# A depthwise convolution moved from TensorE to three other engines in a ternary feed-forward stage

## The chip, the cores and the metric

One Trainium2 chip, one of its cores, one launch. The metric is the device time of that core in microseconds (us), the median of several executions. Engines are TensorE (PE; its weight loads are PEld), VectorE (DVE), ScalarE (ACT), GpSimd (POOL) and SyncE (SP, which only issues transfers here).

## What is computed

Two gated blocks, each a cross attention and a feed-forward, are applied to `x` of 8 rows (batch entries) x 224 tokens x 512. The change is in the first feed-forward, which after a layer norm computes for each row:

```python
def bit_linear(x, w):      # x rounded to 8 bits per token, w to -1, 0, 1
    xq = act_quant(x)      # round(x * s) / s, s = 127 / max|x| of the token
    wq = weight_quant(w)   # clip(round(w / m), -1, 1) * m, m = mean|w|
    return einsum('bsd,hd->bsh', xq, wq)
h = bit_linear(x, w1)                        # 512 -> 2048 channels
h = depthwise_conv1d(h, conv_w, conv_b)      # 3 taps over the tokens, per channel
h = silu(h)
x = x + tanh(g) * bit_linear(h, w2)          # 2048 -> 512
```

## The kernel before

The four stages (attention 0, `bit_ffn`, attention 1, `fp4_ffn`) run one after the other, with `x1`, `x2` and `x3` in device memory between them. Each engine has its own instruction stream in `bit_ffn` (L1346 to L1961), with semaphores between them, and each stream is strictly in the order in which it is written. There is a prologue for row 0 and then nine turns (L1444): turn b does the first half of row b, prepares the input of row b+1 and finishes row b-1. Turn 8 only finishes row 7.

The 2048 hidden channels lie on the 128 partitions in 16 chunks, with the 224 tokens along the free dimension, and go through the engines in 8 groups of two chunks. For group g of row b:

- PE `up_group` (L1892): 2 x 4 bf16 matmuls of 128x224 give the integer product of the ternary `w1q` and the rounded input `xqT`.
- DVE `group` (L1763): two products with the tokens' factors `dB` give `u` in f32.
- PE `conv_group` (L1906): 2 x 3 f32 matmuls with diagonal matrices `taps` (L1919) are the convolution. The profile shows each f32 matmul as two instructions.
- ACT: `t` = conv + bias and `th` = tanh of half of that (L1650, L1651), two chunks each.
- DVE `finish_group` (L1757), two groups later: `h` = (`th` + 1) * `t`, which is twice the Silu. The factor is taken out again in later constants.

Then, per row: DVE `row_maxima` (L1789) reduces `h` over the chunks in three pieces and joins them with maxima; PE turns the 128 maxima per token over (L1956); DVE `row_scales` (L1775) makes the scale of each token; PE (L1888) and ACT (L1669) spread it to all partitions as `sB`; POOL (L1588) multiplies `h` by `sB` in 8 products of two chunks; DVE `round_hidden` (L1795) rounds it to bf16 in two halves; PE's `down` matmuls (L1947) are 32 of 128x512; DVE `add_residual` (L1801, L1807) gives the output.

The input of the next row is prepared in between, by DVE's `PREPARE` (L1722): `row_moments`, `normalise` (which waits for GpSimd's reciprocal roots, `row_roots`, L1549 to L1562), `input_maxima` (L1706 to L1711), `scale_input`, `round_input`, and `row_factors` (L1724). PE turns it over (L1872) and spreads the factors (L1881).

Before and in turn 0 the weights are rounded: ACT takes sums of absolute values (L1604), `total` (L1863) sums them over partitions, ACT and DVE round `w1` (L1607, L1741), POOL and ACT `w2` (L1577, L1664). ACT and POOL also make the diagonal matrices `taps` (L1616, L1571).

## Time and profile before

| | us |
|---|---|
| median of 3 runs | 2177.19 (2176.5 to 2177.56) |
| the profiled execution's own time | 2169.75 |
| its span, first to last instruction | 2168.0 |
| `bit_ffn`, first transfer issued to last residual | 716.1 to 1058.4 |
| `bit_ffn`'s first `up` matmul | 738.6 |
| mean granted TensorE clock | 0.953 |

The page gives each engine's busy time, which is an average over four stages with different limits. Only the stretch from 716 to 1059 us is touched by the change, so the rows below are from there. A line's group shows the idle time of its engine just before it and what ended it. A timeline lists instructions in the order of time, with repeated ones merged (x2 are two of them, and the duration is from the first's start to the last's end).

### The profile page before, as it was taken

The page shows a single profiled execution, that of the slowest core. Times are in us where ns is not written, and L with a number is a line of the kernel's source. Part 1 is how long each engine was busy: PE and PEld are TensorE (multiplying, and loading weights), DVE is VectorE, ACT ScalarE, POOL GpSimd, SP SyncE. Part 2 cuts the span into 40 slices and gives each one's busy share as a digit, 9 for nine tenths or more (in the row PEclk, how much of TensorE's full clock was granted, in tenths as well). Part 3 has the DMA queues.
Part 4 walks back from the last instruction along what each step waited for, and adds up shares of the span by engine and source line. Part 5 has one row for each costly group of instructions (what it writes and reads, how often), then busy time and mean ns, then how long its engine had stood idle before and what let it go on. Part 6 is the DMA issues. An engine that isn't in the chain of part 4 may idle for free. (4 is left out here: it accounts for less than half of the span.)

```text
span 2168.0 us, 42248 instructions
## 1 busy us (share of the span) xinstructions
PE 1926.6 (89%) x15174; PEld 1362.4 (63%) x15208; DVE 1480.5 (68%) x2752; ACT 948.0 (44%) x1305; POOL 1201.2 (55%) x1470
## 2 busy tenths in 40 slices
PE   5799999999987589899489999999999967899997
PEld 3467677777765478778255676767776754455553
DVE  4776776776765588988344666766766456889973
ACT  3176667776777653333123434434434432111110
POOL 3176776766764543323222667767766423877853
PEclk9899999999997799999699999999999988999998
DMA  7445444455420501110452444544543420010100
GB/s 206 106 114 133 113 123 121 117 124 123 115 72 18 198 10 45 31 42 18 153 142 75 115 130 141 148 140 128 149 142 115 161 85 10 30 37 30 34 29 24
DMA packets 184012, 208.67 MB, mean 96 GB/s; under 512 B 61481, under 2 KB 145705, under 8 KB 183337
## 3 DMA queue, kind: packets, MB, share of 16 engines
q1 hardware_dynamic: 183848, 206.46, 33.9%
q8 instruction: 107, 1.75, 0.4%
q14 instruction: 57, 0.46, 0.1%
HBM read 138.61 MB, written 67.53 MB: 95 GB/s over the span
## 5 line engine op out<-in xcount | busy, mean ns | idle before, releaser
L709 POOL TENSOR_TENSOR a_p_hl<-a_p,a_p_hl 125x448 bf16<-125x448 f32 x540 | 562.3, 1043 | 450.2 <-ACT a_p_hl L846 418.5
L836 ACT ACTIVATE a_p<-a_psum 125x1344 f32<-125x1344 f32 x192 | 247.9, 1291 | 135.0 <-PE a_psum L1248 127.9
L1014 DVE TENSOR_REDUCE a_nm<-a_psum 112x1 f32<-112x750 f32 x256 | 237.4, 934 | 98.9 <-PE a_psum L1268 98.3
L846 ACT ACTIVATE a_p_hl<-a_p 125x1344 bf16<-125x1344 f32 x192 | 254.0, 1323 | 81.9 <-PE a_psum L1286 78.3
L1286 PEld LDWEIGHTS a_psum<-a_v_st,a_p_hl 125*128 125x128 bf16 x4608 | 175.2, 98 | 40.5 <-issue 18.5
L1286 PE MATMUL a_psum<-a_v_st,a_p_hl 125*128 125x65 bf16 (+2 forms) x4608 | 186.6, 194 | 12.0 <-POOL a_p_hl L709 6.1
L1919 PE MATMUL f_conv<-f_u,f_taps 128*128 128x224 f32 x768 | 161.1, 359 | 22.4 <-DVE f_u L1771 21.7
L1158 PE MATMUL a_psum<-a_chl,a_w 128*128 128x375 bf16 x768 | 142.4, 331 | 22.8 <-DVE a_w L905 14.9
L1919 PEld LDWEIGHTS f_conv<-f_u,f_taps 128*128 128x128 f32 x768 | 141.6, 191 | 31.8 <-DVE f_u L1771 27.2
L1158 PE MATMUL a_psum<-a_chl,kept_w 128*128 128x375 bf16 x768 | 137.3, 332 | 23.1 <-DVE kept_w L905 18.0
L1268 PE MATMUL a_psum<-a_k_st,a_q_st 96*112 96x375 bf16 x512 | 128.1, 337 | 25.6 <-DVE a_nm L1014 19.0
L1158 PE MATMUL a_psum<-a_w,a_chl 128*125 128x512 bf16 x576 | 139.4, 384 | 8.4 <-DVE a_m_parts L995 5.7
L979 DVE TENSOR_TENSOR a_v_st<-a_psum,a_v_st 125x512 bf16<-125x512 f32 x96 | 66.0, 687 | 110.8 <-ACT a_v_st L814 110.8
L814 ACT ACTIVATE a_v_st<-a_psum 125x512 bf16<-125x512 f32 x96 | 58.3, 608 | 187.4 <-PE a_psum L1158 187.4
L1009 DVE CUSTOM_DVE_ANT_0 a_psum<-a_psum,a_mask_b 112x750 f32<-112x750 f32 x128 | 119.7, 940 | 26.6 <-PE a_psum L1268 25.2
L1158 PE MATMUL a_psum<-kept_w,a_chl 128*125 128x512 bf16 x576 | 134.7, 384 | 3.5 <-DVE a_q_tmp L976 3.4
L2244 POOL TENSOR_TENSOR f_ht<-f_ht,f_hp 128x512 f32<-128x512 f32 (+1 forms) x84 | 99.1, 1207 | 60.9 <-DVE f_hp L1997 59.8
L1268 PE MATMUL a_psum<-kept_k,a_q_st 128*112 128x375 bf16 (+1 forms) x512 | 123.1, 340 | 9.2 <-DMA kept_k<-a_k 4.3
L1650 ACT ACTIVATE f_t<-f_conv,f_cb 128x224 f32<-128x224 f32 x128 | 57.6, 450 | 166.8 <-PE f_conv L1919 166.8
L973 DVE TENSOR_TENSOR a_k_tmp<-a_psum,a_k_tmp 128x375 bf16<-128x375 f32 x128 | 69.7, 545 | 86.9 <-ACT a_k_tmp L807 86.7
L807 ACT ACTIVATE a_k_tmp<-a_psum 128x375 bf16<-128x375 f32 x128 | 61.7, 483 | 139.0 <-PE a_psum L1158 134.3
L1158 PEld LDWEIGHTS a_psum<-a_chl,kept_w 128*128 128x128 bf16 x768 | 73.1, 99 | 74.6 <-issue 34.2
(251 smaller groups left out, 4034.7 us busy)
## 6 DMA issues: line engine op xcount, KB each, us to landing
a_k<-a_k_tmp SPq DMA_DIRECT2D x64, 375.0 KB, 3.0
a_k_st<-a_k SPq DMA_DIRECT2D x96, 187.5 KB, 3.4
kept_k<-a_k SPq DMA_DIRECT2D x96, 187.5 KB, 3.4
a_c<-in_ctx_t SPq DMA_DIRECT2D x16, 750.0 KB, 6.1
ctx_parts<-a_chl SPq DMA_DIRECT2D x16, 750.0 KB, 9.7
a_chl<-ctx_parts SPq DMA_DIRECT2D x16, 750.0 KB, 6.0
a_q_st<-a_q SPq DMA_DIRECT2D x192, 56.0 KB, 2.2
rounded<-a_fw SPq DMA_DIRECT2D x24, 352.0 KB, 3.7
```

The costliest lines, as they stand in the source:

```text
L709: ins = nc.gpsimd.tensor_tensor(p_hl[0:MC, h % 2, 1, cols], p32[0:MC, h % 2, cols], p_hl[0:MC, h % 2, 0, cols], ALU.subtract)
L836: nc.scalar.activation(p32[0:MC, par, :].rearrange("p (b n) -> p b n", b=3), st[0:MC, :, 0:2 * S], ACT.Exp, scale=scale).then_inc(exp_done, 1)
L846: nc.scalar.activation(p_hl[0:MC, par, 0, :], p32[0:MC, par, :], ACT.Copy).then_inc(phi_done, 1)
L973: ins = nc.vector.tensor_tensor(k_tmp[:, cc % 2, 1, cols], bank[:, 0:MK], k_tmp[:, cc % 2, 0, cols], ALU.subtract)
L979: ins = nc.vector.tensor_tensor(v_st[0:MC, b.parity, k, :, DK + 1:VW], bank[0:MC, :].rearrange("p (h d) -> p h d", h=H), v_st[0:MC, b.pari ...
L1009: ins = nc.vector.tensor_tensor_reduce(out=sm_[0:HALF, 0:2, 0:MK], in0=sm_[0:HALF, 0:2, 0:MK], in1=mask_b[:, b.parity, s, :].rearrange("p ...
L1014: ins = nc.vector.tensor_reduce(out, sm_[0:HALF, 0:2, 0:MK], AX.XY, ALU.max, negate=True)
L1158: ins = nc.tensor.matmul(out, lhs, rhs, start=(c == 0 and n == 0), stop=(c == KC - 1 and n == 2))
L1268: ins = nc.tensor.matmul(sm_[0:HALF, kh, 0:MK], q_stack(b.parity, at(h), rows)[:, s * HALF:(s + 1) * HALF], k_stack(b.parity, at(h), rows) ...
L1286: ins = nc.tensor.matmul(ob[:, c0:c0 + width], p_hl[0:MC, h % 2, part, j * S + Q0[s]:j * S + Q0[s] + P], v_st[0:MC, b.parity, j, h, 0:widt ...
L1919: ins = nc.tensor.matmul(conv[:, g % 2, c * S:(c + 1) * S], taps[:, g * GC + c, k, :], u[:, g % 2, c, k:k + S], start=(k == 0), stop=(k == 2))
L2244: ins = nc.gpsimd.tensor_tensor(ht[:, cols], ht[:, cols], hp[:, cols], op)
```

## The change

In `bit_ffn` only:

- The input's values are no longer integers with a factor applied behind the matmul. `xn` is scaled and rounded on ACT (`scale_input`), brought back to its value with `dq` on DVE (`input_values`), and split into a bf16 half (`input_high`, ACT) and the bf16 rest (`input_low`, DVE). Both are turned over on PE (`turn_input`) and copied by ACT (`take_turned`). `up_group` runs both halves, 2 x 8 matmuls. The factors `dB`, their diagonal matmuls (L1881) and `row_factors` are gone.
- The convolution: ACT reads `up` from PSUM twice per chunk (`centre`): `t` = centre tap * `up` + bias, `left` = left tap * `up`. DVE adds the right tap's product in place (`add_right`, two instructions per group, reading `up`). POOL adds `left`, shifted by one token (`add_left`, one instruction per group). The matrices `taps`, `u`, `conv` and L1919 are gone; the taps times the mean of `w1` are `cws`.
- Silu: ACT's own (`silu`, one instruction per group), in place of tanh and `finish_group`.
- `up` has four PSUM banks in place of two. `row_maxima` takes four quarters. POOL's 8 products with `sB` stand between the `add_left` of groups 2 to 7. `row_roots(b+1)` stands behind `add_left(b, 0)` on POOL. ACT's `row_scales(b-1)` stands behind `silu(b, 0)`. PE's turning of the maxima stands behind `up_group(b+1, 0)`, and `down` is run in halves by q, with `turn_input(b+1, 1)` between them.
- At the start `total(0)` stands behind both `turn_input`s on PE, and the first scaling of `w2` is on DVE at the end of turn 0 instead of on POOL.

The diff, cut to its core:

```diff
+            def add_left(b, g):
+
+                pool.wait_ge(right_added, b * NG + g + 1)
+                row = t[:, g % RING, :, 1:S]
+                nc.gpsimd.tensor_tensor(row, row, left[:, g % RING, :, 0:S - 1], ALU.add).then_inc(left_added, 1)
+
+            def scale_hidden(b, par, n):
+
+                if n == 0:
+                    pool.wait_ge(sB_ready, b + 1)
+                part = h[:, par, 2 * n:2 * n + 2, :]
+                ins = nc.gpsimd.tensor_tensor(part, part, sB[:, :].unsqueeze(1).broadcast_to([P, 2, S]), ALU.mult)
+                if n % (QH // 2) < QH // 2 - 1:
+                    own.link(ins)
+                else:
+                    ins.then_inc(h_scaled, 1)
+
+            BEHIND = {2: (0, 1), 3: (2,), 4: (3,), 5: (4, 5), 6: (6,), 7: (7,)}
...
             def turn(b, par):
+                for g in range(NG):
+                    if in_range(b):
+                        add_left(b, g)
+                    if g == 0 and in_range(b + 1):
+                        row_roots(b + 1)
+                    if in_range(b - 1):
+                        for n in BEHIND.get(g, ()):
+                            scale_hidden(b - 1, 1 - par, n)
...
+            def scale_input(b):
+
+                act.wait_ge(inv_ready, b + 1)
+                for s in range(2):
+                    ins = nc.scalar.activation(xn[:, s, :], xn[:, s, :], ACT.Identity, bias=round_sb[0:HALF, 0:1],
+                                               scale=inv[:, s:s + 1])
+                ins.then_inc(xs_ready, 1)
+
+            def input_high(b):
+
+                act.wait_ge(xhat_ready, b + 1)
+                if not (isinstance(b, int) and b == 0):
+
+                    act.wait_ge(xT_ready, b * 2)
+                nc.scalar.activation(xq[:, 0, :, :], xn[:, :, :], ACT.Copy).then_inc(xhi_ready, 1)
...
+            def take_turned(b, part):
+
+                act.wait_ge(xT_ready, b * 2 + part + 1)
+                for s in range(2):
+                    ins = nc.scalar.activation(xqT[:, part, :, s * HALF:(s + 1) * HALF],
+                                               xT_ps[:, s * 512:s * 512 + KC * HALF].rearrange("p (c s) -> p c s", c=KC),
+                                               ACT.Copy)
+                ins.then_inc(xqT_ready, 1)
+
+            def centre(b, g):
+
+                n = b * NG + g
+                if not (isinstance(b, int) and n < RING):
+
+                    act.wait_ge(h_ready, n - RING + 1)
+                act.wait_ge(up_ready, n + 1)
+                for c in range(GC):
+                    ch = g * GC + c
+                    src = up[:, g % BANKS, c * S:(c + 1) * S]
+                    nc.scalar.activation(t[:, g % RING, c, :], src, ACT.Identity, bias=cb[:, ch:ch + 1],
+                                         scale=cws[:, ch, 1:2])
+                    ins = nc.scalar.activation(left[:, g % RING, c, 0:S - 1], src[:, 0:S - 1], ACT.Copy,
+                                               scale=cws[:, ch, 0:1])
+                ins.then_inc(centre_ready, 1)
+
+            def silu(b, par, g):
+
+                if g == 0 and not (isinstance(b, int) and b < 2):
+
+                    act.wait_ge(hq_ready, b * 2)
+                act.wait_ge(left_added, b * NG + g + 1)
+                nc.scalar.activation(h[:, par, g * GC:(g + 1) * GC, :], t[:, g % RING, :, :],
+                                     ACT.Silu).then_inc(h_ready, 1)
...
+            absolute_sum(0, 1, w1q)
+            scale_input(0)
+            absolute_sum(0, 2, w1q)
+            input_high(0)
+            absolute_sum(0, 3, w1q)
...
+            take_turned(0, 0)
+            take_turned(0, 1)
+            act.wait_ge(scale_ready, 1)
+            quantise_w1(ACT_W1[0])
+            quantise_w1(ACT_W1[1])
...
-                for g in range(NG if in_range(b) else 0):
-                    n = b * NG + g
+                for g in range(NG):
+                    if in_range(b):
+                        centre(b, g)
+                    if g >= 2 and in_range(b):
+                        silu(b, par, g - 2)
+                    if g == 2 and in_range(b - 1):
                         row_scales(b - 1)
+                    if g == 4 and in_range(b + 1):
+                        scale_input(b + 1)
+                    if g == 6 and in_range(b + 1):
+                        input_high(b + 1)
+                if in_range(b):
+                    silu(b, par, NG - 2)
                 if in_range(b + 1):
-                    prepare(b + 1)
+                    take_turned(b + 1, 0)
+                if in_range(b):
+                    silu(b, par, NG - 1)
+                if in_range(b + 1):
+                    take_turned(b + 1, 1)
...
+                nc.vector.tensor_scalar(dq[:, :], amax[:, :], 1.0 / 127.0, None, ALU.mult)
                 link(nc.vector.tensor_scalar(inv[:, :], inv[:, :], 127.0, None, ALU.mult))
-
-            def scale_input(b):
+                dve.sem_inc(inv_ready, 1)
...
+            def input_values(b):
+
+                dve.wait_ge(xs_ready, b + 1)
                 for s in range(2):
-                    ins = nc.vector.tensor_scalar(xn[:, s, :], xn[:, s, :], inv[:, s:s + 1], ROUND,
-            PREPARE = {1: row_moments, 2: normalise, 3: input_maxima, 4: scale_input, 5: round_input}
+                    ins = nc.vector.tensor_scalar(xn[:, s, :], xn[:, s, :], -ROUND, dq[:, s:s + 1], ALU.add, ALU.mult)
+                ins.then_inc(xhat_ready, 1)
+
+            def input_low(b):
+
+                dve.wait_ge(xhi_ready, b + 1)
+                nc.vector.tensor_tensor(xq[:, 1, :, :], xn[:, :, :], xq[:, 0, :, :], ALU.subtract).then_inc(xq_ready, 1)
+
+            PREPARE = {0: row_moments, 2: normalise, 3: input_maxima, 5: input_values, 7: input_low}
...
+            def add_right(b, g):
 
                 n = b * NG + g
-                if not (isinstance(b, int) and n < 2):
-
-                    dve.wait_ge(conv_ready, n - 1)
-                dve.wait_ge(up_ready, n + 1)
+                dve.wait_ge(centre_ready, n + 1)
+                if isinstance(b, int) and n == 0:
+                    dve.wait_ge(taps_ready, 1)
                 for c in range(GC):
-                    ins = nc.vector.tensor_tensor(u[:, g % 2, c, 1:S + 1], up[:, g % 2, c * S:(c + 1) * S],
-                                                  dB[:, :], ALU.mult)
-                ins.then_inc(u_ready, 1)
+                    ch = g * GC + c
+                    row = t[:, g % RING, c, 0:S - 1]
+                    ins = nc.vector.scalar_tensor_tensor(row, up[:, g % BANKS, c * S + 1:(c + 1) * S], cws[:, ch, 2:3],
+                                                         row, ALU.mult, ALU.add)
+                ins.then_inc(right_added, 1)
...
+                        for n in range(NG):
+                            w, _ = w2_piece(n)
+                            nc.vector.tensor_scalar(w, w, w_scale[:, 1:2], ROUND, ALU.mult,
+                                                    ALU.add).then_inc(w2_rounded, 1)
+                    if g in (4, 6) and in_range(b):
+                        row_maxima(b, par, g // 2 - 2)
+                    if g == 6 and in_range(b - 1):
+                        round_hidden(b - 1, 1 - par, 0)
                 if in_range(b):
-                    finish_group(b, par, NG - 2)
-                    finish_group(b, par, NG - 1)
-                    link(row_maxima(b, par, 2, QH, FC))
-                    nc.vector.tensor_tensor(hm[:, 0, :], hm[:, 0, :], hm[:, 2, :], ALU.max).then_inc(hm_ready, 1)
+                    link(nc.vector.tensor_tensor(hm[:, 0, :], hm[:, 0, :], hm[:, 1, :], ALU.max))
+                    row_maxima(b, par, 2)
+                if in_range(b - 1):
+                    round_hidden(b - 1, 1 - par, 1)
+                if in_range(b):
+                    link(nc.vector.tensor_tensor(hm[:, 0, :], hm[:, 0, :], hm[:, 2, :], ALU.max))
+                    row_maxima(b, par, 3)
+                    nc.vector.tensor_tensor(hm[:, 0, :], hm[:, 0, :], hm[:, 3, :], ALU.max).then_inc(hm_ready, 1)
                 if in_range(b - 1):
                     add_residual(b - 1)
 
-            row_factors()
+            dve.sem_inc(hq_ready, 2)
...
-                if not (isinstance(b, int) and n < 2):
-                    pe.wait_ge(u_ready, n - 1)
+                if not (isinstance(b, int) and n < BANKS):
+                    pe.wait_ge(right_added, n - BANKS + 1)
...
-                    for k in range(KC):
-                        ins = nc.tensor.matmul(up[:, g % 2, c * S:(c + 1) * S], w1q[:, k, ch * P:(ch + 1) * P],
-                                               xqT[:, k, :], start=(k == 0), stop=(k == KC - 1))
+                    for part in range(2):
+                        for k in range(KC):
+                            ins = nc.tensor.matmul(up[:, g % BANKS, c * S:(c + 1) * S], w1q[:, k, ch * P:(ch + 1) * P],
+                                                   xqT[:, part, k, :], start=(part == 0 and k == 0),
+                                                   stop=(part == 1 and k == KC - 1))
...
+            def hidden_maxima(b):
+
+                if not (isinstance(b, int) and b == 0):
+
+                    pe.wait_ge(sB_ready, b)
+                pe.wait_ge(hm_ready, b + 1)
...
+            def down_half(b, q):
+
+                pe.wait_ge(w2_ready, NG)
+                pe.wait_ge(hq_ready, b * 2 + q + 3)
+                for s in range(2):
+                    for c in range(q * QH, (q + 1) * QH):
+                        ins = nc.tensor.matmul(down[0:HALF, s, :], hqT[:, c, s * HALF:(s + 1) * HALF], w2q[:, c, :],
+                                               start=(c == 0), stop=(c == FC - 1))
+                    if q == 1:
+                        ins.then_inc(down_ready, 1)
 
...
+                for g in range(NG):
+                    if in_range(b):
+                        if g == 0:
+                            pe.wait_ge(xqT_ready, (b + 1) * 2)
+                        up_group(b, g)
+                    if g == 0 and in_range(b - 1):
+                        hidden_maxima(b - 1)
...
                 if in_range(b + 1):
-                    prepare(b + 1)
+                    turn_input(b + 1, 0)
...
+                    down_half(b - 1, 0)
+                if in_range(b + 1):
+                    turn_input(b + 1, 1)
+                if in_range(b - 1):
+                    down_half(b - 1, 1)
+
+            turn_input(0, 0)
+            turn_input(0, 1)
+            total(0)
```

## Rows read from the trace of the kernel before

**Rows 1.** The page, part 1: busy us, share of the span, instructions of each engine

```profile
PE 1926.6 (89%) x15174; PEld 1362.4 (63%) x15208; DVE 1480.5 (68%) x2752; ACT 948.0 (44%) x1305; POOL 1201.2 (55%) x1470
```

**Rows 2.** Windows: us, then busy us of PE, PEld, DVE, ACT, POOL, granted clock

```profile
900.00:940.00 40.00, 36.47 (x227) 31.32 (x225) 35.12 (x60) 14.07 (x40) 14.57 (x22) 1.00 0.12 34
```

**Rows 3.** Lines, 725 to 1060: busy us, mean ns of one, idle before and releaser

```profile
L1919 PE MATMUL f_conv<-f_u,f_taps 128*128 128x224 f32 x768 | 161.1, 359 | 22.4 <-DVE f_u L1771 21.7
L1588 POOL TENSOR_TENSOR f_h<-f_h,f_sB 128x448 f32<-128x448 f32 x64 | 77.5, 1216 | 47.6 <-ACT f_sB L1669 43.8
...
L1902 PE MATMUL f_up<-f_xqT,f_w1q 128*128 128x224 bf16 x512 | 61.2, 267 | 1.0 <-DVE f_w1q L1745 1.0
...
L1792 DVE TENSOR_REDUCE f_hm<-f_h 128x224 f32<-128x896 f32 (+1 forms) x24 | 53.5, 2227 | 0.3
...
L1760 DVE SCALAR_TENSOR_TENSOR f_h<-f_th,f_t 128x448 f32<-128x448 f32 x64 | 45.0, 711 | 1.8 <-ACT f_th L1651 1.4
L1771 DVE TENSOR_TENSOR f_u<-f_up,f_dB 128x224 f32<-128x224 f32 x128 | 43.7, 383 | 13.8 <-PE f_up L1902 10.6
...
L1798 DVE TENSOR_SCALAR f_hqT<-f_h 128x1792 bf16<-128x1792 f32 x16 | 18.2, 1138 | 9.4 <-POOL f_h L1588 9.4
L1702 DVE TENSOR_SCALAR f_xn<-f_xin,f_mv,f_root 112x512 f32<-112x512 f32 x16 | 17.7, 1145 | 18.9 <-POOL f_root L1562 18.9
```

**Rows 4.** Timeline, VectorE at the turns' starts: start, us, instruction, idle before

```profile
778.83 0.69 DVE L1771 TENSOR_TENSOR f_u<-f_up,f_dB 128x224 f32<-128x224 f32 x2 [2.33 <-PE f_up L1902]
...
890.73 0.75 DVE L1807 SCALAR_TENSOR_TENSOR f_xo<-f_down,f_dq,f_xres 112x512 f32<-112x512 f32 x1 [1.29 <-PE f_down L1947]
891.71 0.69 DVE L1771 TENSOR_TENSOR f_u<-f_up,f_dB 128x224 f32<-128x224 f32 x2 [0.23 <-PE f_up L1902]
892.31 0.41 DVE L1778 TENSOR_REDUCE f_hmax<-f_scales_ps 112x2 f32<-112x256 f32 x1
...
1004.10 0.69 DVE L1771 TENSOR_TENSOR f_u<-f_up,f_dB 128x224 f32<-128x224 f32 x2 [0.33 <-PE f_up L1902]
```

**Rows 5.** Timeline, VectorE and GpSimd at once: a normalising pass beside GpSimd's product

```profile
896.48 0.19 POOL L1555 TENSOR_TENSOR f_root<-f_mv,f_root 112x2 f32<-112x2 f32 x1 [24.01 <-DVE f_mv L1696]
...
899.73 1.13 POOL L1588 TENSOR_TENSOR f_h<-f_h,f_sB 128x448 f32<-128x448 f32 x1
...
899.81 1.33 DVE L1702 TENSOR_SCALAR f_xn<-f_xin,f_mv,f_root 112x512 f32<-112x512 f32 x1 [2.31 <-POOL f_root L1562]
```

**Rows 6.** One line's instructions: least, median and most ns, first and last start

```profile
L1709 DVE TENSOR_SCALAR f_amax<-f_amax x8: 169/944/946, 727.4 to 979.9; 112x2 f32<-112x2 f32 x8
```

**Rows 7.** Timeline, ScalarE in one group of a row

```profile
895.03 0.45 ACT L1650 ACTIVATE f_t<-f_conv,f_cb 128x224 f32<-128x224 f32 x1 [9.53 <-PE f_conv L1919]
...
896.03 0.46 ACT L1651 ACTIVATE f_th<-f_conv,f_cb_half 128x224 f32<-128x224 f32 x1
```

**Rows 8.** Timeline, TensorE at a row's end and at the stage's end

```profile
883.61 7.07 PE L1947 MATMUL f_down<-f_w2q,f_hqT 128*112 128x512 bf16 x32
...
890.74 1.70 PE L1902 MATMUL f_up<-f_xqT,f_w1q 128*128 128x224 bf16 x16
...
1045.77 3.63 PE L1947 MATMUL f_down<-f_w2q,f_hqT 128*112 128x512 bf16 x8 [7.39 <-DVE f_hqT L1798]
1050.21 7.37 PE L1947 MATMUL f_down<-f_w2q,f_hqT 128*112 128x512 bf16 x24 [0.81 <-DVE f_hqT L1798]
```

**Rows 9.** Timeline, GpSimd at the stage's end

```profile
1038.85 10.18 POOL L1588 TENSOR_TENSOR f_h<-f_h,f_sB 128x448 f32<-128x448 f32 x8 [19.22 <-ACT f_sB L1669]
```

**Rows 10.** Timeline, start of the stage and end of turn 0, several engines

```profile
733.64 0.19 ACT L1604 ACTIVATION_READ_ACCUMULATOR f_w1q<-f_w 128x1 f32 x1
...
734.35 0.58 PE L1865 MATMUL f_scales_ps<-f_w_sum,f_ones 128*128 128x1 f32 x2 [3.40 <-DVE f_w_sum L1752]
...
736.21 0.75 DVE L1743 TENSOR_SCALAR f_w<-f_w,f_w_scale 128x1024 f32<-128x1024 f32 x1
...
738.61 3.15 PE L1902 MATMUL f_up<-f_xqT,f_w1q 128*128 128x224 bf16 x16 [0.97 <-DVE f_w1q L1745]
...
771.91 8.45 ACT L1664 ACTIVATE f_w2q<-f_w,f_round 128x1024 bf16<-128x1024 f32 x8
```

267 lines of the change are left out of this document (65 added, 202 removed).

## The prediction, made before the changed kernel was run

> **What bounds the kernel now.** The page's busy shares [rows 1] say little here, since four stages are averaged. I first read the window 900 to 940, which is one of `bit_ffn` alone: PE is busy for 36.5 of 40 us and DVE for 35.1, while ACT and POOL have 14 and 15 us [rows 2]. Two engines are near full, so the next view is what each of them waits for. Among the lines, f32 conv is the largest (161 us on PE, where 22 us of idle time ahead of it end with DVE's `u`), and DVE's products wait 11 us for PE [rows 3]. PE waits for DVE more than DVE for PE. Then I read DVE's timeline. From turn 1 (778.83) to turn 7 (1004.10) are six turns in 225.3 us, 37.5 us per row [rows 4]. DVE's gaps in one are 1.29 and 0.23 us at the boundary [rows 4] and 2.31 us before the normalising [rows 5], 3.8 us in all: DVE is working or held for 33.7 of 37.5 us, and is the bound of a row. PE's conv is hidden behind it nearly everywhere.
>
> **How DVE and POOL disturb each other.** Beside POOL's product (899.73, 1.13 us) DVE's pass over 512 elements takes 1.33 us and ends 0.28 us after the product [rows 5]. A pass over two elements takes 169 ns undisturbed, and 944 ns in the median [rows 6]. So such an instruction of DVE waits until the instruction of POOL that has begun is over. A reduction isn't held, nor is one that reads PSUM and one tile: `u` has a mean of 383 ns [rows 3]. That agrees with the Trainium skill (GPSIMD Engine Reference, Key points): GpSimd shares its SBUF interfaces with VectorE's instructions in a 2-port mode or with two SBUF inputs. By that rule `input_low`, the maxima's joins and every `tensor_scalar` from SBUF are held and `add_right` isn't; were nothing held, the row's path below would be 4.0 us shorter.
>
> **PE, per row.** Removed are 96 conv instructions: 161.1/8 less overlap, some 18.5 us. Added are 64 more `up` matmuls; 16 take 1.70 us with their latency [rows 8], so 16 x 8 now take 12.5 us in place of 6.4. PE falls to some 21 us per row. None of this is a gain by itself, since PE wasn't the bound.
>
> **ACT, per row.** Four instructions of a group take 0.33 us each from start to start (895.03 to 896.49, 1.46 us) [rows 7]. `centre` is four again. `silu`, on 448 elements, lies between 0.45 and two such, 0.8 us; I take 0.55. With the input's scaling, high half, four copies and `sB`, ACT has 8 x (1.35 + 0.55) + 5 = 20 us. Not a bound.
>
> **DVE, per row.** Gone are `u` (43.7/8 = 5.5 us), `finish_group` (45.0/8 = 5.6), the factors and one rounding (some 2.5). New are `add_right`, 16 instructions of the size of `u` (383 ns [rows 3]; up to 450 with a scalar pointer), some 6 us; `input_low` on 1024 elements, bounded by the 711 ns of 448 [rows 3] on the scale of size at 1.6, and taken at 1.25; two more joins; the input's values in place of its scaling. Maxima are 53.5/8 = 6.7 us as before [rows 3]. Undisturbed that is 33.7 - 13.6 + 6.0 + 1.25 + 0.9, less some 3 us of holding that is in the 33.7: 25 us. But POOL now has 16 products and the roots in place of 8 and the roots. Some 12 instructions of DVE meet it: two normalising passes, three small ones of the maxima, two of the values, low half, joins, rounding. At 0.3 to 1.1 us each that is 5 to 10 us, I take 8: 33 us, where it was.
>
> **POOL, per row, and the path that sets the period.** Eight products take 10.18 us [rows 9], 1.25 us each, so POOL has 16 x 1.25 + 3.3 (roots, 896.48 to 899.78 [rows 5]) = 23.3 us. That is well below the period, but most of it is in series. In the new order, from `add_right(b, 0)`:
>
> - `add_right` 0.75, then `row_scales` and the moments: 892.31 to 896.48, less one `u` pair, is 3.5 [rows 4, 5]; a hold by `add_left(b, 0)` 0.7. Sum 4.95. POOL has gone on to `row_roots(b+1)` and waits for the moments, with `add_left(b, 1)` and all scaling of row b-1 queued behind.
> - Roots 3.3, to 8.25.
> - Seven `add_left` and eight `scale_hidden`: 15 x 1.25 = 18.8, to 27.0.
> - POOL held by DVE in turn (the first half's rounding alone is 1.0 us), or waiting for `add_right(b, 4)` behind `input_maxima`: bounds 0 and 5, I take 3.3, to 30.3.
> - The second half's rounding, 1.1 [rows 3], to 31.4.
> - PE: 16 `down` matmuls. 32 take 7.07 [rows 8], so 3.5. Then `up_group(b+1, 0)`, 1.7, which stands behind them in PE's queue; `centre` 1.46; semaphores 0.2. Sum 6.9, to 38.3.
>
> Before, `up_group(b+1, 0)` stood behind `down` too, but `down` hardly waited for a rounding: both halves were rounded before the last maxima. Now this piece is in the path. DVE has the last maxima and the residual (some 4.5 us) within those 6.9, and idles for the rest. I add 0.2 for the clock, below: **38.5 us per row against 37.5**. Bounds: 34.3 with no holds on this path, 44 with PE at its lower clock in both pieces.
>
> **Start and turn 0.** Before, ACT's last sum of `w1` ends at 733.8, `total(0)` starts at 734.35, DVE rounds `w1` from 736.21, the first `up` is at 738.61 [rows 10]. The 24 + 24 tap matrices on ACT and POOL go away, but the sums waited for their transfers anyway. New on ACT ahead of the last sum: `input_high`, behind DVE's first reduction and values (some +0.9). New ahead of `total(0)`: `take_turned(0, 0)` (1.0) and the second turning over (0.9 at the low clock). Less `row_factors`: first `up` some 2 us later. `up` itself then has 16 matmuls in place of 8 per chunk pair, 3.2 us at the low clock as in 738.61's row, before the first `centre`. In turn 0 ACT has its groups (8 x 1.9), the two `w1` pieces, four sums, the input's and eight signs of `w2` (8.45 [rows 10]): I lay them one after the other from 744.0 and reach 784.7. DVE's scaling of `w2` (8 x 0.75, now in front of its last maxima) ends its turn at 786.3. Before, turn 1 starts at 778.83; now at 786.4: **+7.6**, bounds +3 and +12.
>
> **Turn 7 and the end.** Turn 7 prepares nothing, so the roots and held passes fall away: 28.6 against 31.4, **-2.8**. In turn 8, half of `down` is done for both token halves before the last rounding: 16 matmuls behind it in place of 24, **-1.5** as the clock is low there. ACT also needs its table for Silu and back; one load or two, hidden or 3 us, inside the bounds.
>
> **Sum.** +7.6 + 6 x 1.0 - 2.8 - 1.5 = +9.3, say **+9**. The profiled execution, 2169.75, lies 7.4 below the median of 2177.19; on the profile's scale 2178.8, on the median's **2186.2**.
>
> **Clock.** After 7.4 us of idleness 8 `down` matmuls take 3.63 us, 0.44 each, against 0.22 in the row; the next 24 take 7.37, still partly slow [rows 8]. So idle time costs PE its 2.4 GHz here, for 1.2 GHz, and it takes several us of work to get it back. In the new order PE has run ahead by four banks at some 13 us of a row and then waits for the first rounding at some 25 us, with only 8 transposes between: its next work, `down`'s first half, starts at 1.2 GHz. That half has slack (25 + 6 = 31, the second starts at 31.4). The Trainium skill says the same (TensorE: Matmul & The Clock Gate, Why this matters for your kernels): idle gaps between bursts throw the clock back. By it the second half and `up` may also be slow, the third rival.
>
> **Rivals.**
> - *Relief counts* (faster): DVE's holds fall between POOL's instructions and the path has none of the 3.3 and 0.7: period 35.5 (the bound of 34.3 and a third of the holds). 6 x -2 + 3.3 = -9: 2168. For it: DVE's undisturbed work is 25 us, PE's is nearly halved. Against: every pass beside POOL in the old trace is held. It decides below 37.0 us per row. Chance 0.22.
> - *Nothing per row* (the same): period 37.5 as the joint of DVE and POOL stays where it was, and turn 0 is cheaper (ACT's signs and DVE's scaling overlap with turn 1): +0 to +4, about 2179. Chance 0.16.
> - *PE's clock*: both pieces on the path at 1.2 GHz, 3.5 + 1.7 us more per row, 43.7: 6 x 6.2 + 3.3 = +40: 2217 in full, some 2205 if in half the rows. For it: idle gaps of 8 us in each row. Against: the first half of `down` warms PE just before. Chance 0.12.
> - The forecast, 2181.6 to 2195: chance 0.50.
>
> **How the numbers follow.** The rival cases are faster 0.20 and same 0.02 of the first, same 0.16 of the second, slower 0.12 and 0.50: faster by over 0.2% 0.20, same 0.18, slower 0.62 (0.2%, 4.4 us, is about what a measurement of this kernel can tell from no change). The range leaves out the first rival's lower third and the clock's full cost: 2165 to 2209.
>
> **What would show it.** DVE's row starts 38.5 us apart (35.5: first rival; 43: third); normalising passes and low half of over 1 us beside POOL; POOL idle in front of `row_roots` and then without gaps; 7 us from the end of the second rounding to the next `add_right`; PE's clock below 1.00 in a row's second half; turn 1 starting some 8 us later. The forecast is wrong if DVE waits elsewhere: for `silu` before a quarter's maxima, or for ACT's scaling.

## The result, and the profile of the changed kernel

The changed kernel takes 2183.02 us (median of 20 runs), the kernel before 2176.85 (20 runs beside them): a ratio of 1.0028, 95% interval 1.0016 to 1.0040, or +6.2 us. The forecast was +9, to 2186.2. The profiled execution has a span of 2181.3 us against 2168.0. `bit_ffn` accounts for 7.5 of those 13.3; the stage also begins 2.1 us later in the trace, behind unchanged code, and the last 3.7 lie behind it, where nothing was changed either.

The page's busy line of each engine, to be held against [rows 1]:

```profile
PE 1847.0 (85%) x14984; PEld 1278.5 (59%) x14984; DVE 1467.2 (67%) x2696; ACT 1009.1 (46%) x1378; POOL 1256.3 (58%) x1501
```

TensorE has lost 80 us of busy time and the kernel is slower. The window of one row (us, then busy us of PE, PEld, DVE, ACT, POOL, and the granted clock) says why that is possible; [rows 2] is its counterpart:

```profile
907.60:945.10 37.50, 23.85 (x185) 18.89 (x183) 30.31 (x50) 21.42 (x48) 23.06 (x27) 0.86 0.13 37
```

No engine is full, and the row takes 37.5 us as before. VectorE's timeline of the same row, with the first add of turns 1 and 7 around it (start, us, instruction, idle before):

```profile
795.66 0.81 DVE L1794 SCALAR_TENSOR_TENSOR f_t<-f_up,f_cws,f_t 128x223 f32<-128x223 f32 x2 [1.51 <-ACT f_left L1647]
...
907.62 0.81 DVE L1794 SCALAR_TENSOR_TENSOR f_t<-f_up,f_cws,f_t 128x223 f32<-128x223 f32 x2 [2.46 <-ACT f_left L1647]
908.35 0.41 DVE L1801 TENSOR_REDUCE f_hmax<-f_scales_ps 112x2 f32<-112x256 f32 x1
908.80 0.87 DVE L1803 TENSOR_SCALAR f_hmax<-f_hmax 112x2 f32<-112x2 f32 x1
...
915.99 2.60 DVE L1730 TENSOR_SCALAR f_xn<-f_xin,f_mv,f_root 112x512 f32<-112x512 f32 x2 [2.04 <-POOL f_root L1556]
...
936.76 1.09 DVE L1822 TENSOR_SCALAR f_hqT<-f_h 128x1792 bf16<-128x1792 f32 x1 [0.36 <-POOL f_h L1574]
...
941.87 0.75 DVE L1831 SCALAR_TENSOR_TENSOR f_xo<-f_down,f_dq,f_xres 112x512 f32<-112x512 f32 x1 [0.88 <-PE f_down L1942]
945.08 0.81 DVE L1794 SCALAR_TENSOR_TENSOR f_t<-f_up,f_cws,f_t 128x223 f32<-128x223 f32 x2 [2.46 <-ACT f_left L1647]
...
1020.18 0.81 DVE L1794 SCALAR_TENSOR_TENSOR f_t<-f_up,f_cws,f_t 128x223 f32<-128x223 f32 x2 [2.52 <-ACT f_left L1647]
```

Six rows from 795.66 to 1020.18 are 224.5 us, 37.4 each; before they were 37.5 [rows 4]. VectorE waits for the roots (2.04), for GpSimd's last product (0.36), for `down` (0.88) and for the next row's first group (2.46). GpSimd and TensorE in that row:

```profile
912.63 0.20 POOL L1549 TENSOR_TENSOR f_root<-f_mv,f_root 112x2 f32<-112x2 f32 x1 [2.99 <-DVE f_mv L1724]
...
915.91 2.40 POOL L1567 TENSOR_TENSOR f_t<-f_t,f_left 128x446 f32<-128x446 f32 x2
...
935.59 1.14 POOL L1574 TENSOR_TENSOR f_h<-f_h,f_sB 128x448 f32<-128x448 f32 x1
```

```profile
932.32 5.66 PE L1942 MATMUL f_down<-f_w2q,f_hqT 128*112 128x512 bf16 x16 [2.34 <-DVE f_hqT L1822]
937.81 0.56 PE L1898 MATMUL f_xT_ps<-f_ident_b,f_xq 112*128 112x112 bf16 x8
938.21 3.62 PE L1942 MATMUL f_down<-f_w2q,f_hqT 128*112 128x512 bf16 x16
941.66 1.70 PE L1920 MATMUL f_up<-f_xqT,f_w1q 128*128 128x224 bf16 x16
```

From the roots on GpSimd has gaps of 1.3 us in all until its last product; then second rounding (to 937.85), second half of `down`, `up_group(b+1, 0)`, first group: the forecast's path. The first half of `down` ran at the lower clock: 16 matmuls in 5.66 us, the next 16 in 3.62.

Where the time went, counted from the stage's first transfer (716.10 before, 718.20 after). Up to turn 7 a turn starts at its first add, behind that at the reduction of the maxima, 0.6 us later before and 0.7 after, so that the pieces sum to 7.3:

| piece | before | after | change | forecast |
|---|---|---|---|---|
| to the first `up` | 22.5 | 24.55 | +2.0 | +2 |
| from there to turn 1's first add | 40.2 | 52.9 | +12.7 | +5.6 |
| six rows | 225.3 | 224.5 | -0.8 | +6.0 |
| turn 7 | 31.4 | 27.0 | -4.4 | -2.8 |
| turn 8 | 22.3 | 20.1 | -2.2 | -1.5 |

### The profile page after: what moved, and what is told of

The parts are those of the page before. It is cut to its first block and busy times, and to the rows that moved or that the text cites. A ratio compares the mean times of both kernels' runs of the same rounds, so it can differ in the third digit from the quotient of the medians.

```text
span 2181.3 us, 41913 instructions
## 1 busy us (share of the span) xinstructions
PE 1847.0 (85%) x14984; PEld 1278.5 (59%) x14984; DVE 1467.2 (67%) x2696; ACT 1009.1 (46%) x1378; POOL 1256.3 (58%) x1501
## 5 line engine op out<-in xcount | busy, mean ns | idle before, releaser
L1158 PE MATMUL a_psum<-a_chl,a_w 128*128 128x375 bf16 x768 | 142.6, 332 | 22.3 <-DVE a_w L905 14.5
L1158 PE MATMUL a_psum<-a_chl,kept_w 128*128 128x375 bf16 x768 | 137.3, 331 | 27.1 <-DVE kept_w L905 18.6
L1567 POOL TENSOR_TENSOR f_t<-f_t,f_left 128x446 f32<-128x446 f32 x64 | 82.9, 1300 | 116.1 <-DVE f_t L1794 113.0
L1009 DVE CUSTOM_DVE_ANT_0 a_psum<-a_psum,a_mask_b 112x750 f32<-112x750 f32 x128 | 119.8, 941 | 28.6 <-PE a_psum L1268 27.1
L1920 PE MATMUL f_up<-f_xqT,f_w1q 128*128 128x224 bf16 x1024 | 111.5, 271 | 16.2 <-DVE f_t L1794 11.6
L1248 PE MATMUL a_psum<-a_q_st,kept_k 128*125 128x224 bf16 (+1 forms) x768 | 119.0, 261 | 0.0
```

Of the source, the lines that this page charges most:

```text
L1009: ins = nc.vector.tensor_tensor_reduce(out=sm_[0:HALF, 0:2, 0:MK], in0=sm_[0:HALF, 0:2, 0:MK], in1=mask_b[:, b.parity, s, :].rearrange("p ...
L1158: ins = nc.tensor.matmul(out, lhs, rhs, start=(c == 0 and n == 0), stop=(c == KC - 1 and n == 2))
L1248: ins = nc.tensor.matmul(out, k_stack(b.parity, at(h), rows)[:, j * MC:(j + 1) * MC], q_stack(b.parity, at(h), rows), start=(t == 0 and no ...
L1920: ins = nc.tensor.matmul(up[:, g % BANKS, c * S:(c + 1) * S], w1q[:, k, ch * P:(ch + 1) * P], xqT[:, part, k, :], start=(part == 0 and k = ...
```

## The experiments

Each is one profiled execution, except the last. Whole times of one kernel differ by more than most of these edits are worth (2169.9 to 2188.4 us in the 20 runs of the kernel before), so what is compared is the length of the pieces in the traces. A turn's start is taken from here on at `row_scales`' reduction of the maxima (`f_hmax`, L1801 in the kernel after). From first `up` to turn 1 that is 40.8 us before and 53.6 after; the mean of the six rows 37.55 and 37.42.

**total_late.** Where did turn 0 lose 7 us more than forecast? TensorE's and ScalarE's timelines of the kernel after:

```profile
776.00 0.59 PE L1887 MATMUL f_scales_ps<-f_w_sum,f_ones 128*128 128x1 f32 x2 [17.70 <-DVE f_w_sum L1847]
776.45 3.10 PE L1920 MATMUL f_up<-f_xqT,f_w1q 128*128 128x224 bf16 x16
```

```profile
779.66 0.54 ACT L1645 ACTIVATE f_t<-f_up,f_cb,f_cws 128x224 f32<-128x224 f32 x1 [3.20 <-PE f_up L1920]
...
785.69 8.42 ACT L1709 ACTIVATE f_w2q<-f_w,f_round 128x1024 bf16<-128x1024 f32 x8
```

`total(1)` stands in TensorE's queue in front of `up_group(0, 7)`. It waits 17.7 us for the sum of `w2`'s absolute values. ScalarE works on for most of that, then waits 3.20 us for the group of `up` behind it, and the rest of its turn with it.

```
-                    if g == 6 and isinstance(b, int) and b == 0:
+                    if g == NG - 1 and isinstance(b, int) and b == 0:
                         total(1)
```

> The changed kernel, with total(1), the sum of w2's absolute values over the partitions, behind up_group(0, 7) on PE instead of in front of it. In the changed kernel PE waits there for 17.7 us, and up_group(0, 7) then runs at the low clock (776.45 to 779.55). Theory (part of what turn 0 costs is this place in PE's queue): ACT's centre(0, 7) no longer waits its 3.2 us, and turn 1 starts 3 to 4 us earlier after the stage's first transfer: 74 instead of 77.5 us. Rival (ACT's own work sets turn 0's end, the wait is covered by the signs of w2): turn 1 starts at 77 us. The rows behind keep 37.4 us in both.

Measured: turn 1 starts 48.9 us after the first `up`, 4.7 less; its first add 72.4 us after the first transfer (722.42), where the theory had 3 to 4 us off 77.5. The rows take 37.7. Not all of the 4.7 us is the edit's. Windows of TensorE's second group of `up` in the kernel after and in total_late:

```profile
745.90:749.00 3.10, 3.10 (x20) 2.51 (x19) 1.33 (x3) 1.77 (x5) 0.44 (x1) 0.55 0.22 63
```

```profile
749.73:752.83 3.10, 3.10 (x34) 3.10 (x33) 1.34 (x3) 3.01 (x8) 0.45 (x1) 1.00 0.11 44
```

In the kernel after this group ran at a granted clock of 0.55, and ScalarE waited 1.24 us for it. It was so in up_first, busy_up_first and w2_off_path too, and not in total_late nor in four other runs with the same turn 0 (skip_two_products, pe_kept_busy and the two with half the maxima), where turn 1 starts 52.2 to 52.3 us after the first `up`. Against these total_late gains 3.3 us, inside the theory's 3 to 4. So of the 7.1 us the wait of `total(1)` cost 3.3, and the clock at the second group 1.3. What decides whether that group is slow was not tried.

**w2_on_pool.** The eight scalings of `w2` leave VectorE for GpSimd.

```
-                            nc.vector.tensor_scalar(w, w, w_scale[:, 1:2], ROUND, ALU.mult,
-                                                    ALU.add).then_inc(w2_rounded, 1)
...
+                        nc.gpsimd.tensor_scalar(w, w, w_scale[:, 1:2], ROUND, ALU.mult,
+                                                ALU.add).then_inc(w2_rounded, 1)
```

> The changed kernel with the first scaling of w2 on GpSimd, as in the kernel before, instead of on VectorE ahead of the last maxima. Theory (ACT's eight signs are last in turn 0, and they wait for the scaled pieces): VectorE is free 5.5 us earlier, but the pieces come 1.25 us apart instead of 0.7, so ACT's signs end 1 to 2 us later, and turn 1 starts at 78 to 79 us after the stage's first transfer instead of 77.5. Rival (VectorE is last): turn 1 starts 5 us earlier, at 72.

Measured: 52.9 us. The second group of `up` was fast here, so this goes beside 52.3 and not 53.6: 0.6 us later, the theory's direction at less than its 1 to 2 us. VectorE was now ready 7.0 us before turn 1's first add and waited for ScalarE, whose signs of `w2` (8.98 us, 8.31 before) came last. VectorE's scaling was a second leg that ended 1.5 us ahead of ScalarE's in the kernel after, and no bound alone.

**w2_off_path.** Both legs at once, on total_late. So that the signs can stand in turn 1, turns 1 and 2 are written out on all engines.

```
             turn(0, 0)
-            with engine_loop(0, (B - 2) // 2) as i:
+            turn(1, 1)
+            turn(2, 0)
+            with engine_loop(0, (B - 4) // 2) as i:
...
+                    if isinstance(b, int) and b == 1 and 1 <= g < 5:
+                        for n in (2 * g - 2, 2 * g - 1):
+                            act.wait_ge(w2_rounded, n + 1)
...
```

> The edit is made on the kernel of the run total_late: turns 1 and 2 are written out, the eight signs of w2 go on ScalarE two by two behind groups 1 to 4 of turn 1, and GpSimd, not VectorE, scales w2. Theory: turn 0 has two legs to turn 1 of nearly the same length, ScalarE's signs (8.4 us, 784.84 in total_late) and VectorE's scaling (5.55 us, 783.11), so that each alone bought nothing (w2_on_pool: -0.8 us); with both off the way, turn 1's first sum of VectorE comes 5.5 us earlier, 43.4 us after the first `up` in place of 48.9 in total_late, and the later rows stay at 37.5. Rival: a third leg (GpSimd's 9.2 us of scaling in front of the first `add_left` of turn 1, or the matmuls of `up` for turn 1) takes its place at once: 47 to 49 us.

Measured: 45.4 us, 3.6 of the 5.5 expected. 1.2 of the missing 1.9 are ScalarE's wait for the second group of `up`, slow here (a granted clock of 0.57) and not in total_late. ScalarE now also waits 3.32 us for `up_group(1, 0)`, a third leg through the low half's turning over. But turns 1 and 2 took 40.9 and 40.5 us, and the kernel got slower, 2191.0. Turn 2, VectorE (both passes as one entry, then the first alone) and GpSimd:

```profile
842.42 4.77 DVE L1738 TENSOR_SCALAR f_xn<-f_xin,f_mv,f_root 112x512 f32<-112x512 f32 x2 [2.03 <-POOL f_root L1558]
842.42 3.50 DVE L1738 TENSOR_SCALAR f_xn<-f_xin,f_mv,f_root 112x512 f32<-112x512 f32 x1 [2.03 <-POOL f_root L1558]
```

```profile
842.34 2.21 POOL L1569 TENSOR_TENSOR f_t<-f_t,f_left 128x446 f32<-128x446 f32 x2
844.50 2.40 POOL L1576 TENSOR_TENSOR f_h<-f_h,f_sB 128x448 f32<-128x448 f32 x2
```

In the loop the same two passes take 2.60 us (915.99 above) and GpSimd's pair 2.40: they alternate, one pass to a product. Written out, GpSimd's pair takes 2.21. VectorE's first pass takes 3.50 us and ends 0.3 us behind GpSimd's third product (844.50 + 1.13), the second 1.3 us. Turn 2 has no signs of `w2`, so they alone are not the reason; the last run has more on it.

**up_first.** Is `up_group(b+1, 0)` behind `down` on the path? It is put ahead of the second half of `down`.

```
                     turn_input(b + 1, 1)
+                    pe.wait_ge(xqT_ready, (b + 2) * 2)
+                    up_group(b + 1, 0)
                 if in_range(b - 1):
                     down_half(b - 1, 1)
```

> The changed kernel with up_group(b+1, 0) in front of the second half of row b-1's down matmuls on PE, instead of behind it. Theory (the row's period is the path POOL - second rounding - down - up - centre - add_right): after the rounding only VectorE's last maxima, the down half and the residual remain, add_right follows the residual at once, and the 2.46 us in front of it go away: 34.9 to 35.3 us per row instead of 37.4. Rival (VectorE's and POOL's work sum up to the row whatever PE does): the wait appears in another place, 37 us.

Measured: 37.5 us per row, no gain, as the rival had it. TensorE's timeline:

```profile
931.74 5.44 PE L1942 MATMUL f_down<-f_w2q,f_hqT 128*112 128x512 bf16 x16 [2.34 <-DVE f_hqT L1822]
937.02 0.56 PE L1898 MATMUL f_xT_ps<-f_ident_b,f_xq 112*128 112x112 bf16 x8
938.72 1.70 PE L1920 MATMUL f_up<-f_xqT,f_w1q 128*128 128x224 bf16 x16 [1.15 <-ACT f_xqT L1630]
940.26 3.62 PE L1942 MATMUL f_down<-f_w2q,f_hqT 128*112 128x512 bf16 x16
```

The slow first half of `down` holds up the second turning over, that the moved `up`, and that the second half of `down`, which starts 32.5 us behind the row's start in place of 29.9. That the moved step is on the path all the same, and that the clock hides it, is shown further down by busy_up_first.

**moments_first.** On VectorE the moments come ahead of `row_scales`, so that GpSimd's roots, and all that is queued behind them, start earlier.

```
-                    if g == 0 and in_range(b - 1):
-                        row_scales(b - 1)
                     if g in PREPARE and in_range(b + 1):
                         PREPARE[g](b + 1)
+                    if g == 0 and in_range(b - 1):
+                        row_scales(b - 1)
```

> The changed kernel with the moments of row b+1 in front of row_scales on VectorE instead of behind it. Theory (GpSimd waits for the moments with all its work of the row queued behind): the roots start some 2.6 us earlier after the row's first add_right (2.4 instead of 5.0), and as GpSimd's chain is the path, the row becomes up to 2.5 us shorter: 35 to 35.5 us. Bound from the scales: they come 1.6 us later, at about 4.6 us, still ahead of GpSimd's first product. Rival (VectorE's own work bounds the row): 37.4, the wait is given back in front of the second rounding.

Measured: 35.3, 34.8, 36.6, 34.9 and 36.7 us from row to row. By the first adds, which the edit leaves in place, the mean of six is 35.5 against 37.4, at 2170.3 us in all. The path through the roots is confirmed: they start 2.5 us behind the first add in place of 5.0. In the short rows the second rounding starts 26.7 us behind the first add, where it was 29.1, nearly the full 2.5. In the two long rows it starts at 27.8. ScalarE waits there 2.3 to 2.5 us behind `sB` for its group of `up`, where it waits 1.2 to 1.9 in the short ones, and the first half of `down` takes 6.2 to 6.3 us in place of 5.4 to 5.6. That points at TensorE's clock; in combined, at 1.00, every looped row has 26.7. One row by VectorE:

```profile
904.43 0.81 DVE L1794 SCALAR_TENSOR_TENSOR f_t<-f_up,f_cws,f_t 128x223 f32<-128x223 f32 x2 [2.46 <-ACT f_left L1647]
...
907.19 0.17 DVE L1803 TENSOR_SCALAR f_hmax<-f_hmax 112x2 f32<-112x2 f32 x1
...
910.35 2.60 DVE L1730 TENSOR_SCALAR f_xn<-f_xin,f_mv,f_root 112x512 f32<-112x512 f32 x2 [0.28 <-POOL f_root L1556]
```

The wait for the roots fell from 2.04 to 0.28 us, and the two-element L1803 takes 0.17 us where it took 0.87 beside `add_left`.

**before_one_tap.** Was TensorE a bound before? Two of three taps are left out of the kernel before.

```
-                    for k in range(3):
+                    for k in range(1, 2):
```

> The kernel before with only the middle tap's matmuls of the convolution: 64 of its 96 matmul instructions of a row are left out, so the outer taps are not added. Theory, VectorE bounds a row of the kernel before (33.7 of 37.5 us): TensorE's busy time falls by 12 us a row, and the row takes 36.5 to 37.5 us. Rival, TensorE with its 36.5 of 40 us bounds it: 31 to 33 us.

Measured: 37.58 us per row against 37.55. Windows of one row of it, and of the kernel before:

```profile
886.50:924.10 37.60, 27.65 (x150) 20.40 (x147) 32.64 (x58) 13.07 (x36) 12.21 (x19) 0.82 0.13 37
```

```profile
891.71:929.20 37.49, 34.25 (x214) 29.45 (x212) 32.69 (x58) 13.05 (x36) 12.21 (x19) 1.00 0.13 37
```

TensorE's busy time falls by 6.6 us, not 12, as its granted clock falls from 1.00 to 0.82; VectorE has the same 32.7 us and the row the same length. The slower clock doesn't hide a gain at the row's end: VectorE's wait for `down` there grows from 1.28 to 1.42 us only. Relief of TensorE was worth nothing in a row. In turn 7 it was: 25.4 us in place of 31.4.

**skip_two_products.** Two of GpSimd's eight products by the scale are left out of each row, so a quarter of the hidden values stays unscaled.

```
-            BEHIND = {2: (0, 1), 3: (2,), 4: (3,), 5: (4, 5), 6: (6,), 7: (7,)}
+            BEHIND = {2: (0,), 3: (2,), 4: (3,), 5: (4,), 6: (6,), 7: (7,)}
```

> The kernel after with two of GpSimd's eight products by the row's scale (numbers 1 and 5) left out of each row, so that a quarter of the hidden values stays unscaled. Theory, the period is set by the chain moments, roots, GpSimd's queue, second rounding, second half of down: the queue is 2 x 1.26 us shorter, so 34.9 us per row in place of 37.4. Rival, VectorE sets the period as its own work: two fewer instructions to be held by, 0.5 us at most, so 36.9 or more.

Measured: 37.67 us, the rival's number. The second rounding starts 27.9 us behind the row's start in place of 28.4, so the 2.5 us became 0.5. GpSimd now waits for VectorE's sums instead, 1.21, 0.71 and 1.74 us in one row, the last of them in front of its last two products:

```profile
969.88 2.35 POOL L1567 TENSOR_TENSOR f_t<-f_t,f_left 128x446 f32<-128x446 f32 x1 [1.74 <-DVE f_t L1794]
```

In the same stretch of the kernel after only one such wait is over 0.2 us (0.68). So VectorE's queue ends just some 0.5 us ahead of GpSimd's. The 0.5 us were then lost to the first half of `down`, 6.05 us here. Three ends lie within half a microsecond: GpSimd's queue, VectorE's, and TensorE's slow half. The next run takes the third away.

**pe_kept_busy.** 92 matmuls per row without a use fill TensorE's two gaps ahead of `down`.

```
+                if in_range(b) and in_range(b - 1):
+                    for _ in range(72):
+                        nc.tensor.matmul(scales_ps[:, 2 * P + 2:2 * P + 2 + S], w1q[:, 0, 0:P], xqT[:, 0, 0, :],
+                                         start=True, stop=True)
...
+                        for _ in range(20):
+                            nc.tensor.matmul(scales_ps[:, 2 * P + 2:2 * P + 2 + S], w2q[:, 0, 0:P], w2q[:, 0, 0:S],
+                                             start=True, stop=True)
```

> The kernel after with 72 matmuls without a use behind the last `up` group of a row and 20 more ahead of the first half of down, written into an unused part of the scales' bank, so that TensorE does not idle for 8 and 2.3 us there. Theory: the first half of down takes 3.6 us in place of 5.7, but what stands behind it starts only 0.4 us late in the kernel after (second half at 938.21, its rounding ends 937.85), so 37.0 to 37.1 us per row in place of 37.4, and a granted clock above 0.97. Rival, the low clock is what costs the new kernel its gain: 35.5 us or less.

Measured: 37.26 us per row at a granted clock of 1.00.

```profile
931.92 3.66 PE L1942 MATMUL f_down<-f_w2q,f_hqT 128*112 128x512 bf16 x16 [0.79 <-DVE f_hqT L1822]
935.42 0.56 PE L1898 MATMUL f_xT_ps<-f_ident_b,f_xq 112*128 112x112 bf16 x8
937.52 3.66 PE L1942 MATMUL f_down<-f_w2q,f_hqT 128*112 128x512 bf16 x16 [1.55 <-DVE f_hqT L1822]
```

The first half takes 3.66 us, and TensorE then waits 1.55 us for the second rounding. The gain is 0.2 (0.3 to 0.4 was expected): the clock alone costs the kernel after next to nothing, as the forecast's slack for it said.

**busy_up_first.** Both edits together.

> The edits of pe_kept_busy and of up_first together. up_first alone gained nothing (37.5 us per row), as the low-clock first half of down pushed the second turning over, and with it the moved up_group(b+1,0), to where the second half of down had to wait for it; pe_kept_busy alone took 37.26. Theory: with the first half of down at 3.66 us, the second turning over is over at 936.0 in pe_kept_busy's row (907.95 to 945.24), up_group(b+1,0) runs from 936.9 to 938.6 beside the second rounding, the second half of down ends at 942.2 and VectorE's next sum follows the residual at 943.0 in place of 944.4: 35.7 to 36.1 us per row, so the two together give what neither gives alone. Rival, VectorE and GpSimd hold the row at 37.2 whatever TensorE does.

Measured: 35.81 us per row, inside the expected 35.7 to 36.1, where the two alone gained 0.2 and nothing. The clock hid what the order of TensorE's queue was worth.

**busy_half_maxima and busy_half_maxima_skip.** Which of VectorE and GpSimd paces the stretch from the roots to the second rounding? On pe_kept_busy, VectorE's maxima are taken over half of each quarter (the row's scale is not the true one), first alone, then with the two products left out.

```
-  h[:, par, at * quarter:(at + 1) * quarter, :]
+  h[:, par, at * quarter:at * quarter + quarter // 2, :]
```

> pe_kept_busy, and VectorE's maxima of the first three quarters of a row taken over half of each quarter's channels only (the row's scale is then not the true one): 0.85 us less of VectorE's work three times, all before the second rounding. In pe_kept_busy the stretch from the roots to the second rounding is a queue on both engines: VectorE idles 1.5 us in it and GpSimd 1.3. Theory, GpSimd's 15 products and VectorE's work are both full there: GpSimd's queue does not get shorter, so only its waits for VectorE go, 36.5 to 36.8 us per row in place of 37.26. Rival, VectorE alone paces the row: 34.7 to 35.2.

> As busy_half_maxima, and two of GpSimd's eight products by the row's scale left out, as in skip_two_products (which alone gained 0 to 0.2 us per row). Theory, both queues between the roots and the second rounding get 2.5 us shorter, so the row does: 34.7 to 35.2 us in place of 37.26, more than the two edits bring apart. Rival, another wait (ScalarE's chain for the next row's input, the first half of down) holds the row at 36.2 or more.

Measured: 37.2 us in four rows of busy_half_maxima and 38.7 in two. VectorE's second rounding in it, at a row that starts at 830.24:

```profile
858.66 1.09 DVE L1822 TENSOR_SCALAR f_hqT<-f_h 128x1792 bf16<-128x1792 f32 x1 [2.75 <-POOL f_h L1574]
```

That is 28.4 us behind the row's start, exactly as in pe_kept_busy; VectorE only waits 2.75 us there in place of 0.35. With all its products GpSimd's queue is the later end, and the theory's 0.5 to 0.8 us for its waits did not come either. In the two long rows the second half of `down` took 5.20 and 5.06 us in place of 3.66. TensorE has the same gap of 2.52 us ahead of it in the short rows, so why two rows of six were slow is open. With the products left out too the second rounding starts at 27.1 us, 1.3 earlier, where the two edits brought 0 and 0.5 alone. The rows are 35.89 us, 1.4 less, where 2.1 to 2.6 were expected. VectorE's timeline shows the rest:

```profile
916.08 0.81 DVE L1794 SCALAR_TENSOR_TENSOR f_t<-f_up,f_cws,f_t 128x223 f32<-128x223 f32 x2 [1.60 <-ACT f_left L1647]
```

It waits 1.60 us for a group that stands in ScalarE's queue behind `scale_input`, which itself waits for VectorE's `input_maxima`: a third path through the same stretch. What leaving out two products would bring with VectorE's maxima whole and the clock high was not tried.

**combined.** All edits that the runs point to, with the whole computation; only ScalarE's turns 1 and 2 are written out. `total(0)` also goes ahead of the second turning over.

> The kernel after with the edits that the other runs point to, all of them with the whole computation: total(1) behind up_group(0,7) and total(0) behind the first turning over; w2 scaled on GpSimd and its eight signs on ScalarE in turn 1, for which ScalarE's turns 1 and 2 alone are written out (in w2_off_path all engines' were, and both turns took 3 us longer, with the two normalising passes at 4.8 us in place of 2.6); the moments ahead of row_scales; up_group(b+1,0) ahead of the second half of down; TensorE kept busy by 92 matmuls without a use per row. Theory, the gains add up as they take from different pieces of the row: 1.8 (moments_first) and 1.6 (busy_up_first) us per row from 37.4, so 34.0; turn 1 starts 44 us after the first `up` in place of 53.6; a span of 2181.3 - 6 x 3.4 - 9 = 2152 us, a ratio to the kernel before of 0.985 to 0.993. Rival, the two gains of a row are one and the same wait, so 35.3 to 35.8 us per row and a ratio of 0.992 to 0.999; a third, that turns 1 and 2 take 40.5 us here too, as GpSimd's and VectorE's order in them comes from the signs and not from the written-out code.

Measured in 6 runs of it against 11 of the kernel before: 2153.9 against 2175.6 us, a ratio of 0.9908, interval 0.9884 to 0.9932. The span is 2145.4 us. The window of one row, and VectorE at its end:

```profile
890.00:923.34 33.34, 30.10 (x276) 26.55 (x274) 29.70 (x51) 21.20 (x49) 23.15 (x27) 1.00 0.15 42
```

```profile
920.25 0.75 DVE L1848 SCALAR_TENSOR_TENSOR f_xo<-f_down,f_dq,f_xres 112x512 f32<-112x512 f32 x1 [0.91 <-PE f_down L1955]
920.92 0.80 DVE L1811 SCALAR_TENSOR_TENSOR f_t<-f_up,f_cws,f_t 128x223 f32<-128x223 f32 x2
```

Rows 2 to 5 take 33.34 us, and by the first adds the mean of six is 34.1 (34.0 expected); the next row's first add follows the residual with no wait. So the two gains per row add up, and in these rows to 4.1 us, more than 1.9 and 1.6. It is the 2.5 by which the roots start earlier, plus 1.6, as if the clock no longer took its part from the rows of moments_first. Turn 1's first add (782.90) is 44.2 us behind the first `up` (738.74), 8.7 less than the 52.9 of the kernel after, where the theory had 9.6 less (44 in place of 53.6). Turn 1 itself takes 38.0 us, as its signs of `w2` hold `add_right` up by 2.9 us. Its two normalising passes take 2.60 us, with the signs there and VectorE and GpSimd in their loop. So the third rival did not come, and the 4.8 us of w2_off_path do not come from the signs; they go with the written-out form of these two engines' turns (the moments' place differs too). What in that form does it was not tried.

## Why the prediction held, and where it did not

**What bounded the kernel before: right that it was not TensorE.** With a third of the convolution's matmuls the row is as long as with all (before_one_tap), so moving them away could bring nothing in a row. That VectorE is the bound was not tried by taking work from it alone. The prediction counted 33.7 us of it per row from three gaps; the window of a row has 32.7 busy. In the kernel after its 33 us came to 30.3.

**The path of a row: right in its steps.** From the first add to the roots 4.95 us were laid out; measured 5.01 (907.62 to 912.63). Roots over at 8.25, measured 8.3. Second rounding over to the next add 6.9, measured 7.2 (937.85 to 945.08). Moving the moments took 1.9 us off the row, and putting `up` ahead took off 1.4 once the clock allowed it. GpSimd's queue is the middle of the path by a narrow margin: VectorE's relief alone left the second rounding at 28.4 us, but GpSimd's relief by 2.5 us moved it by 0.5 only, since VectorE's queue is next. The prediction had such waits for VectorE in its term for holding and waits.

**The size of its middle: the term that was off.** I took 15 products at 1.25 us and 3.3 us of holding and waits on top, to 30.3. Measured is 29.1 (last product over at 936.73). From the roots' end on it is 20.8 us: beside the 18.8 of the products, 3.3 should have been 2.0. Undisturbed, they start 1.09 us apart (1032.18, 1033.27, 1034.36 in turn 7), 16.4 for 15; then 1.3 us are waits and 3.1 holding. Of the holding 2.4 were already in the 1.25, a mean over eight products of which VectorE had lengthened one (to 1.86 us). So the row came to 37.4, not 38.5, and the six rows to -0.8 in place of +6.0. The row went as the rival "nothing per row" had it, while the sum came out near the forecast. That was luck: an error of 7 us in turn 0 stands against one of 7 us in the six rows and one of 2 at the end, of opposite sign.

**Turn 0: the step that failed.** I laid ScalarE's work end to end and got +7.6 for turn 1's start, where +14.7 came: 40.7 us for ScalarE's stretch (744.0 to 784.7), 48.0 measured (745.99 to 794.00). 5.7 us are waits. The largest, 3.20, is that of `total(1)`: a wait in TensorE's queue in front of a group of `up` that ScalarE needs, and total_late gives 3.3 back. The prediction added up ScalarE's work and did not ask what stands ahead of its input in TensorE's queue. 1.24 us are the second group of `up` at the low clock, which was laid out for the first group only, and 1.26 a wait for GpSimd's `add_left` ahead of the last `silu`. Some 1.9 us more are ScalarE's own instructions. A group of four takes 1.5 us and `silu` 0.48 from start to start, where 1.35 and 0.55 were used, 0.6 us in eight groups; the table for Silu was loaded once, 1.28 us, in the open. Four lines of the kernel after:

```profile
L1645 ACT ACTIVATE f_t<-f_up,f_cb,f_cws 128x224 f32<-128x224 f32 x128 | 69.3, 542 | 40.6 <-PE f_up L1920 40.0
L1647 ACT ACTIVATE f_left<-f_up,f_cws 128x223 f32<-128x223 f32 x128 | 58.0, 453 | 0.0
L1657 ACT ACTIVATE f_h<-f_t 128x448 f32<-128x448 f32 x64 | 37.7, 591 | 39.3 <-POOL f_t L1567 39.3
L1657 ACT ACT_TABLE_LOAD x1 | 1.3, 1283 | 0.0
```

With scale and bias both per partition, L1645 costs 542 ns; with one of the two L1647 costs 453. The Trainium skill (ScalarE: Activation LUTs, What ACT_TABLE_LOAD costs) gives about 93 ns for each pointer operand and about 1283 ns for the load. The rows agree, 89 and 1283 ns.

**Turn 7 and the end: right in sign, short by 2.3 us.** Turn 7 took 27.0 us against 28.6 laid out. GpSimd's 15 products went through in 18.0 us there (1024.18 to 1042.19) without a wait, so here too 18.8 and 3.3 were too much; the prediction doesn't show how the 28.6 is put together, so the account stops there. In turn 8 the stretch behind the last rounding is 6.0 us (1061.93 to 1067.96) where it was 8.2, with 16 matmuls in it in place of 24: 2.2 less against 1.5 laid out.

**The clock: right for the kernel as it stands.** The first half of `down` runs mostly at 1.2 GHz (5.66 us for 16, against 3.62 for the next 16) and costs 0.2 us per row, the amount that was added. The third rival, with both pieces on the path slow, did not come: 3.62 and 1.70 us are full speed. (Its price at half the rows adds up to 2202, not 2205.) What was not foreseen is that the same slow half cancels the worth of a better order. The matmuls without a use show it from the other side: a clock of 1.00 and 3.66 us. The rule of the Trainium skill cited ahead of the result (TensorE: Matmul & The Clock Gate, Why this matters for your kernels), that idle gaps between bursts throw the clock back, agrees with the slow first half; what the prediction drew from it for the second half and `up` did not come.

**The price of two engines meeting: right.** `L1803`, of two elements, takes 0.87 us beside `add_left` and 0.17 without it (moments_first). The Trainium skill (GPSIMD Engine Reference, Key points) names contention between the two engines for VectorE's instructions in a 2-port mode or with two inputs in SBUF. `L1803` has one such input, so it could only be of the first kind; no row shows an instruction's mode, but the 0.70 us that it loses agree.
